# Embedding gathers on GpSimd: a memset between them against a wait for every fourth landing

## Chip, cores, metric

One core of a Trainium2 chip runs the kernel. The metric is the device time of one execution in microseconds (us). Engines are named as in the profile: PE is TensorE (PEld its weight loads), DVE is VectorE, ACT is ScalarE, POOL is GpSimd, SP is SyncE, which only issues DMAs here.

## What is computed

```python
e = jnp.stack([tbl_f[ids[:, f]] for f in range(32)], axis=1)   # [2048, 32, 64] fp32
gram = jnp.einsum('bnd,bmd->bnm', e, e)                         # 32 x 32 products a sample
z = gram[:, rows, cols]                                         # the 496 pairs above the diagonal
h = jnp.concatenate([z, dense_ctx], axis=1)                     # [2048, 512]
h = jnp.maximum(h @ W_top1 + b_top1, 0.0)                       # 512 -> 512
h = jnp.maximum(h @ W_top2 + b_top2, 0.0)                       # 512 -> 256
y = h @ W_top3                                                  # 256 -> 1
```

The 32 tables have 1000, 1250, 12500 or 125000 rows of 64 floats (256 bytes).

## The kernel before

The batch of 2048 is cut into 8 supers (`SUPERS`) of 256 samples, each of two tiles of 128. The 32 fields are sorted into slots by table size. Slots 0 to 15 (`LOOKED_UP`, `UNITS` = 16) have small tables: they stand in SBUF, and each field of a super is looked up on PE, as a product of a one-hot matrix with the table (`look_up`, L303). DVE makes the one-hot matrix (`make_onehot`, L495, a comparison of two fp16 inputs) and adds the three parts of the result (`add_parts`, L503). Slots 16 to 31 are gathered from HBM by GpSimd: one indirect DMA brings 128 rows of 256 bytes, one a partition, so a field of a super takes two. In super 0 slots 12 to 15 are gathered too. That makes 40 gathers for super 0 and 32 for each of the seven others, 264 in all, in the order super, slot, tile, written out without a loop register. All of them are issued by one function, `gather` (L247 to L260), on GpSimd's own instruction stream, which does nothing else until the last 6 moves of cells at the end (L192).

The looked-up and the gathered rows of a super lie in `rows`, which has two halves, for even and odd supers. Slots form 8 groups of 4; a gathered group has 8 gathers (4 slots of 2 tiles) and a semaphore for each half, `rows_landed[parity][group]`, to which each gather adds 16 as it lands. PE's `transpose_group` (L289) waits for the group's whole count. From super 2 on, GpSimd waits ahead of the first gather of each group until the transposes of two supers earlier have been drained (`turned_drained`).

In each step PE transposes the 8 groups of super s, with look-ups for super s + 1 between them, then makes 8 batches of pair products (`gram_batch`, L316), with more look-ups between them and the three layers (L328, L338, L345) of super s - 1. ACT drains the transposes (L404) and the first half of each batch (L441); DVE drains the second half (L530). In the first 60 us DVE and ACT also split the small tables into three bf16 parts (L539, L544, L450), while SP loads those tables. The last super has no look-ups beside it, and after it the layers of the last two supers stand alone.

Between two gathers stands a memset of `pause`, 128 x 384 floats that nobody reads. It adds one to the semaphore `paused`; before it stands a wait until the memset before has been counted.

Of the kernel before, what the change touches and what calls it, by code (L numbers as in the profile page):

```python
# [10 lines left out]
P = 128  # L11
# [9 lines left out]
GROUP_F = 4  # L21
GROUPS = FIELDS // GROUP_F
# [30 lines left out]
READY_MADE = 3  # L53
assert READY_MADE < RING and READY_MADE <= UNITS and not any(GRAM_UNITS[GRAM_BATCHES - READY_MADE + 1:])
SP_MOVES = 10
PAUSE = 384
MOVES = [(i, jq) for i in range(QUAD) for jq in range(QUAD)]
LAYER1_BEFORE, LAYER2_BEFORE, LAYER3_BEFORE = (4, 5), 6, 7

# [31 lines left out]
def build(nc, ids, tables, dense, w1, b1, w2, b2, w3, identity, second, looked_ids, codes, out):  # L91
    fp32, i32, bf16, fp16 = mybir.dt.float32, mybir.dt.int32, mybir.dt.bfloat16, mybir.dt.float16
# [4 lines left out]
    with ctx:  # L97
        def sb(name, shape, dt):
            return ctx.enter_context(nc.sbuf_tensor(name, shape, dt))
# [4 lines left out]
        def sem(name):  # L104
            return ctx.enter_context(nc.semaphore(name))
# [6 lines left out]
        h1 = sb("h1", [P, OT1, SUPER], fp32)  # L112
        h2 = sb("h2", [P, OT2, SUPER], fp32)
        y = sb("y", [1, BATCH], fp32)
        pause = sb("pause", [P, PAUSE], fp32)
        w1_sb = sb("w1_sb", [P, CHUNKS, HIDDEN1], fp32)
        w2_sb = sb("w2_sb", [P, OT1, HIDDEN2], fp32)
        w3_sb = sb("w3_sb", [P, OT2], fp32)
# [30 lines left out]
        rows_landed = [[sem(f"rows_landed_{p}_{g}") for g in range(GROUPS)] for p in range(2)]  # L149
# [31 lines left out]
        onehot_ready = sem("onehot_ready")  # L181
        lookup_ready = sem("lookup_ready")
        looked_up = sem("looked_up")
        paused = sem("paused")
        folds_begun = sem("folds_begun")
        block = ctx.enter_context(nc.Block())

# [3 lines left out]
        def move_cells(engine, i, jq, parity):  # L191
            return engine.dma_start(pairs[FIELDS * jq:FIELDS * (jq + 1), parity, i],  # L192
                                    folded[FIELDS * i:FIELDS * (i + 1), i, CHUNKS * jq:CHUNKS * (jq + 1), :])
# [48 lines left out]

        @block.gpsimd
        def _(pool):
            pauses = count()

            def gather(s, begin=UNITS):  # L247
                for slot in range(begin, FIELDS):
                    f = SLOT_FIELD[slot]
                    if s >= 2 and (slot == begin or slot % GROUP_F == 0):  # L250
                        pool.wait_ge(turned_drained, EMPTY + GROUPS * (s - 2) + slot // GROUP_F + 1)
                    for t in range(TILES):
                        nc.gpsimd.indirect_dma_start(  # L253
                            rows[:, s % 2, slot, t, :], None, tables[f][:, :],
                            bass.IndirectOffsetOnAxis(index[:, s, t, f:f + 1], 0),
                        ).then_inc(rows_landed[s % 2][slot // GROUP_F], 16)
                        before = next(pauses)
                        if before:
                            pool.wait_ge(paused, before)
                        nc.gpsimd.memset(pause[:], 0.0).then_inc(paused, 1)  # L260

            pool.wait_ge(first_index_loaded, 16)
            gather(0, begin=FIRST_UNITS)
            pool.wait_ge(index_loaded, 16)
            for s in range(1, SUPERS):
                gather(s)
            pool.wait_ge(second_copied, GRAM_EMPTY + GRAM_BATCHES * SUPERS)
            for i, jq in MOVES[SP_MOVES:]:
                move_cells(pool, i, jq, 1).then_inc(moved_by_pool, 16)
# [340 lines left out]
```

## Time and profile before

| | |
|---|---|
| median of 3 runs | 508.75 us (504.62 to 510.11) |
| profiled execution, its own time | 506.08 us |
| its span, first to last instruction | 504.3 us |
| busy: PE, DVE, ACT, POOL | 423.6, 297.8, 114.6, 417.8 us |
| gathers on POOL (L253) | 264, 299.4 us |
| memsets on POOL (L260) | 264, 115.7 us |

A busy time is a sum over the instructions of an engine. The span is what the rows of the trace cover; the execution's own time is 1.8 us longer. All durations of the argument come from that one execution, whose own time lies 2.7 us below the median.

### The profile page before, as it was taken

Reading aid. Unit: us, or ns where it says so; the run is one execution under the profiler, and the core shown is the slowest. Engines: PE = TensorE matmul, PEld = TensorE weight load, DVE = VectorE, ACT = ScalarE, POOL = GpSimd, SP = SyncE. Lnnn points to the kernel's source line nnn. Section 1 sums busy time; section 2 is a strip of 40 time slices with the busy share of each in tenths; the row PEclk is TensorE's granted clock in tenths of the full one; section 3 lists DMA queues with packets and bytes.
Section 4 is the critical chain, followed back from the end, with each engine's and each line's share of the span. In section 5 each row is a group of like instructions: output and inputs, shape, how many; then the busy total and the mean of one; then the engine's idle time right before and its main releaser. Section 6 shows DMA issues by size and latency. Waiting matters only on the chain.

```text
span 504.3 us, 10183 instructions
## 1 busy us (share of the span) xinstructions
PE 423.6 (84%) x4080; PEld 382.6 (76%) x4080; DVE 297.8 (59%) x361; ACT 114.6 (23%) x206; POOL 417.8 (83%) x538
## 2 busy tenths in 40 slices
PE   5398589995299989979799969988999959993887
PEld 5387479984298879869698869868897949883765
DVE  2599779794094589448483749339753948250400
ACT  2244312131011321123012311132103300230311
POOL 7999999998898899888998989889998899885010
PEclk9699799997599999999799979999899979996999
DMA  4444631012301122112301123112311231111010
GB/s 109 140 141 149 205 137 22 17 33 51 102 15 23 25 60 98 22 26 61 102 17 24 40 57 88 22 27 56 102 21 21 54 84 44 24 35 44 1 43 2
DMA packets 22070, 29.58 MB, mean 59 GB/s; under 512 B 9910, under 2 KB 14198, under 8 KB 20896
## 3 DMA queue, kind: packets, MB, share of 16 engines
q1 hardware_dynamic: 12980, 18.96, 10.9%
q0 software_dynamic: 8640, 8.86, 10.7%
q10 hardware_dynamic: 404, 1.09, 0.5%
q8 instruction: 37, 0.61, 0.5%
q14 instruction: 9, 0.07, 0.0%
HBM read 24.61 MB, written 0.07 MB: 49 GB/s over the span
## 4 chain that ended last, share of the span: by engine, by line
POOL 82%; issue 9%; PE 4%; DMA 2%; SPq 1%; DVE 1%; ACT 1%; DVEq 0%; ACTq 0%
POOL rows L253 59%; POOL pause L260 23%; PE mlp_ps L328 1%; PE gram_ps L316 1%; SPq L192 1%; PE mlp_ps L338 1%; DVE folded L530 1%; ACT folded L441 0%; DMA rows<-tbl,index 0%; PE gram_ps L352 0%; SPq L219 0%; DMA index<-ids 0%; DMA pairs<-dense 0%; DMA pairs<-folded 0%; PE turn_ps L289 0%
## 5 line engine op out<-in xcount | busy, mean ns | idle before, releaser
L253 POOL DMA_INDIRECT rows<-tbl,index x264 | 299.4, 1134 | 45.9 <-issue 43.3
L303 PE MATMUL turn_ps<-split_sb,onehot 125*128 125x192 bf16 x2192 | 210.4, 256 | 19.9 <-DVE split_sb L544 17.3
L303 PEld LDWEIGHTS turn_ps<-split_sb,onehot 125*128 125x128 bf16 x2192 | 192.9, 102 | 27.8 <-DVE split_sb L544 18.7
L495 DVE TENSOR_TENSOR onehot<-place,codes_wide 125x2048 bf16<-125x2048 f16 (+1 forms) x127 | 168.1, 1325 | 7.3 <-DMA place<-ids_scratch 7.3
L260 POOL MEMSET pause<- 128x384 f32 x264 | 115.7, 438 | 0.2
L503 DVE TENSOR_REDUCE rows<-turn_ps 128x128 f32<-128x384 f32 x124 | 68.8, 556 | 70.8 <-PE turn_ps L303 68.1
L530 DVE COPY_PREDICATED folded<-second_sb,gram_ps 128x512 f32<-128x512 int32 x64 | 46.6, 729 | 81.8 <-ACT folded L441 81.7
L316 PE MATMUL gram_ps<-emb_t 64*128 64x128 f32 x1024 | 74.0, 286 | 3.3 <-DVE folded L530 3.3
L316 PEld LDWEIGHTS gram_ps<-emb_t 64*128 64x128 f32 x1024 | 62.7, 190 | 17.7 <-issue 13.3
L289 PE MATMUL mlp_ps<-ident_sb,rows 128*128 128x128 f32 x240 | 39.1, 288 | 40.8 <-DMA rows<-tbl,index 34.5
L441 ACT COPY folded<-gram_ps 128x512 f32<-128x512 f32 x64 | 37.5, 586 | 152.0 <-PE gram_ps L316 152.0
L289 PEld LDWEIGHTS mlp_ps<-ident_sb,rows 128*128 128x128 f32 x240 | 27.7, 147 | 43.9 <-issue 41.7
L404 ACT COPY emb_t<-mlp_ps 128x512 f32<-128x512 f32 x58 | 34.0, 586 | 114.3 <-PE mlp_ps L289 106.1
L328 PE MATMUL mlp_ps<-pairs,w_sb 128*128 128x256 f32 x256 | 58.5, 383 | 1.1 <-DMA pairs<-dense 1.1
L328 PEld LDWEIGHTS mlp_ps<-pairs,w_sb 128*128 128x128 f32 x256 | 47.5, 190 | 8.3 <-DMA pairs<-dense 1.6
L352 PE MATMUL gram_ps<-ident_sb 128*128 128x128 f32 x192 | 29.2, 316 | 4.3 <-DMA ident_sb<-identity 4.3
L352 PEld LDWEIGHTS gram_ps<-ident_sb 128*128 128x128 f32 x192 | 26.8, 167 | 4.3 <-DMA ident_sb<-identity 4.3
L338 PE MATMUL mlp_ps<-h,w_sb 128*128 128x256 f32 x128 | 29.6, 384 | 0.0
L421 ACT ACTIVATE h<-mlp_ps,b_sb 128x256 f32<-128x256 f32 x32 | 13.4, 471 | 60.0 <-PE mlp_ps L328 60.0
L338 PEld LDWEIGHTS mlp_ps<-h,w_sb 128*128 128x128 f32 x128 | 23.7, 190 | 3.8
L486 DVE COPY y<-mlp_ps 1x256 f32 (+1 forms) x8 | 5.0, 620 | 23.3 <-PE mlp_ps L345 23.3
L192 POOL DMA_DIRECT2D pairs<-folded x6 | 3.0, 525 | 17.2 <-DVE folded L530 17.2
(28 smaller groups left out, 75.8 us busy)
## 6 DMA issues: line engine op xcount, KB each, us to landing
place<-ids_scratch SPq DMA_DIRECT2D x8, 1000.0 KB
rows<-tbl,index POOLq DMA_INDIRECT x264, 2.7
pairs<-folded SPq DMA_DIRECT2D x122, 32.0 KB
emb_t<-tbl SPq DMA_DIRECT2D x8, 250.0 KB
folded<-tbl SPq DMA_DIRECT2D x5, 312.5 KB
w_sb<-w SPq DMA_DIRECT2D x1, 1024.0 KB
place<-ids_scratch ACTq DMA_DIRECT2D x1, 750.0 KB
rows<-tbl SPq DMA_DIRECT2D x2, 312.5 KB
```

The source lines that it names most:

```text
L253: nc.gpsimd.indirect_dma_start(rows[:, s % 2, slot, t, :], None, tables[f][:, :], bass.IndirectOffsetOnAxis(index[:, s, t, f:f + 1], 0),). ...
L260: nc.gpsimd.memset(pause[:], 0.0).then_inc(paused, 1)
L289: last = nc.tensor.transpose(turn_bank[g % banks][:, k, :], rows[:, parity, GROUP_F * g + k].rearrange("p t d -> p (t d)"), ident_sb[:])
L303: last = nc.tensor.matmul(turn_ps[:, u % 2].rearrange("p k b -> p (k b)")[:, t * PARTS * DIM:(t + 1) * PARTS * DIM], onehot[:, u % RING, c ...
L316: last = nc.tensor.matmul(gram_ps[:, k % 2, t, u // TILES].rearrange("p h ij -> p (h ij)"), e.rearrange("p b f -> p (b f)"), e.rearrange(" ...
L328: last = nc.tensor.matmul(mlp_ps[:, o // 2, o % 2, :], w1_sb[:, jj, P * o:P * (o + 1)], pairs[:, parity, :, jj, :], start=(jj == 0), stop= ...
L338: last = nc.tensor.matmul(mlp_ps[:, 0, o, :], w2_sb[:, k, P * o:P * (o + 1)], h1[:, k, :], start=(k == 0), stop=(k == OT1 - 1))
L352: nc.tensor.transpose(gram_ps[:, 0, 0].rearrange("p u h ij -> p (u h ij)")[:, 0:P], ident_sb[:], ident_sb[:])
L441: nc.scalar.copy(folded[:, :, :, BATCH_Q * k:BATCH_Q * (k + 1)].rearrange("p i j (q t) -> p (i j) q t", t=TILES), gram_ps[:, k % 2, :, :, ...
L495: nc.vector.tensor_tensor(onehot[:, u % RING, 0:SPAN[u], :], place[:, parity, u, :].unsqueeze(1).to_broadcast([TP, SPAN[u], SUPER]), codes ...
L503: nc.vector.reduce_sum(rows[:, parity, u, :, :], turn_ps[:, u % 2].rearrange("p k b -> p (k b)")[:, 0:TILES * PARTS * DIM] .rearrange("p ( ...
L530: nc.vector.copy_predicated(folded[:, :, :, BATCH_Q * k:BATCH_Q * (k + 1)].rearrange("p i j (q t) -> p (i j) q t", t=TILES), second_sb[:]. ...
```

## The change

The memset, its tile and its semaphore are gone. GpSimd counts its gathers, and behind every fourth (`AT_ONCE`) it waits until the group's semaphore has all that has been issued to it so far. As every group has 8 gathers, the four gathers behind one another always belong to one group, and the wait asks for the landing of all four. There are 66 such waits, 10 in super 0 and 56 behind it.

```diff
-PAUSE = 384
+AT_ONCE = 4
...
-        pause = sb("pause", [P, PAUSE], fp32)
...
-        paused = sem("paused")
...
-            pauses = count()
+            issued = count()
+            landed = [[0] * GROUPS for _ in range(2)]
...
                         ).then_inc(rows_landed[s % 2][slot // GROUP_F], 16)
-                        before = next(pauses)
-                        if before:
-                            pool.wait_ge(paused, before)
-                        nc.gpsimd.memset(pause[:], 0.0).then_inc(paused, 1)
+                        group = slot // GROUP_F
+                        landed[s % 2][group] += 1
+                        if next(issued) % AT_ONCE == AT_ONCE - 1:
+                            pool.wait_ge(rows_landed[s % 2][group], 16 * landed[s % 2][group])
```

## Rows read from the trace of the kernel before

**Rows 1.** The page: chain that ended last, shares of the span by engine and line

```profile
POOL 82%; issue 9%; PE 4%; DMA 2%; SPq 1%; DVE 1%; ACT 1%; DVEq 0%; ACTq 0%
```

**Rows 2.** The chain in order of time: start, us, what; its begin and its last gather

```profile
0.75 1.95 DMA index<-ids
2.70 0.29 issue
2.99 1.15 POOL rows L253
...
459.62 2.36 DMA rows<-tbl,index
461.98 0.04 issue
462.02 1.12 PE turn_ps L289 x4
```

**Rows 3.** The page, costliest groups: busy us, mean ns, idle before and its releaser

```profile
L253 POOL DMA_INDIRECT rows<-tbl,index x264 | 299.4, 1134 | 45.9 <-issue 43.3
L260 POOL MEMSET pause<- 128x384 f32 x264 | 115.7, 438 | 0.2
L192 POOL DMA_DIRECT2D pairs<-folded x6 | 3.0, 525 | 17.2 <-DVE folded L530 17.2
```

**Rows 4.** PE's waits from 75 to 470 us: us in total, times, longest us

```profile
PE mlp_ps L289 <- DMA rows<-tbl,index: 34.5, 7, 10.8
PE turn_ps L289 <- DMA rows<-tbl,index: 7.7, 1, 7.7
```

**Rows 5.** PE's wait for rows in two stretches, 180:190 and 350:356 us

```profile
PE mlp_ps L289 <- DMA rows<-tbl,index: 2.4, 1, 2.4
...
PE mlp_ps L289 <- DMA rows<-tbl,index: 2.3, 1, 2.3
```

**Rows 6.** Timeline of POOL, a stretch without DVE one-hots: start, us, instruction, [idle before]

```profile
321.33 0.95 POOL L253 DMA_INDIRECT rows<-tbl,index  x1 [0.17 <-issue]
322.28 0.43 POOL L260 MEMSET pause<- 128x384 f32 x1
322.88 0.95 POOL L253 DMA_INDIRECT rows<-tbl,index  x1 [0.17 <-issue]
```

**Rows 7.** Timeline of DVE and POOL from 141 to 147 us, large one-hots

```profile
141.04 1.48 DVE L495 TENSOR_TENSOR onehot<-place,codes_wide 125x2560 bf16<-125x2560 f16 x1
141.48 0.43 POOL L260 MEMSET pause<- 128x384 f32 x1
142.08 1.27 POOL L253 DMA_INDIRECT rows<-tbl,index  x1 [0.16 <-issue]
...
143.80 1.48 DVE L495 TENSOR_TENSOR onehot<-place,codes_wide 125x2560 bf16<-125x2560 f16 x1
143.94 2.16 POOL L253 DMA_INDIRECT rows<-tbl,index  x1 [0.17 <-issue]
```

**Rows 8.** Timeline of POOL: first and last of 81 gathers behind 75 us over 1.06 us

```profile
80.31 1.16 POOL L253 DMA_INDIRECT rows<-tbl,index  x1 [0.17 <-issue]
...
425.13 1.27 POOL L253 DMA_INDIRECT rows<-tbl,index  x1 [0.17 <-issue]
```

**Rows 9.** Gathers of super 0 and then of the others, by tile: min/median/max

```profile
L253 POOL DMA_INDIRECT rows<-tbl,index x40: 950/961/2032, 3.0 to 73.9; - x40
DMA to landing us min/median/max: 3.9/4.6/6.2
...
L253 POOL DMA_INDIRECT rows<-tbl,index x224: 950/952/2258, 75.5 to 459.6; - x112
DMA to landing us min/median/max: 2.3/2.5/3.6
```

**Rows 10.** L253 by windows: stretch, POOL busy (gathers), TensorE clock, DMA share, GB/s

```profile
0.00:75.00 75.00, 47.61 (x40) 0.89 0.47 148
75.00:461.00 386.00, 251.82 (x224) 0.94 0.20 46
```

**Rows 11.** Timeline of DVE and POOL from 343 us, one one-hot of 1.2 us a turn

```profile
343.20 1.21 DVE L495 TENSOR_TENSOR onehot<-place,codes_wide 125x2048 bf16<-125x2048 f16 x1
343.48 0.43 POOL L260 MEMSET pause<- 128x384 f32 x1
344.08 1.16 POOL L253 DMA_INDIRECT rows<-tbl,index  x1 [0.17 <-issue]
...
344.96 1.22 DVE L495 TENSOR_TENSOR onehot<-place,codes_wide 125x2048 bf16<-125x2048 f16 x1
345.24 0.43 POOL L260 MEMSET pause<- 128x384 f32 x1
345.84 1.16 POOL L253 DMA_INDIRECT rows<-tbl,index  x1 [0.17 <-issue]
```

## Prediction

> **What bounds the kernel now.** I read the chain that ended last first: 82% of the span is POOL and 9% issue, PE only 4% [rows 1]. Its parts in order of time show what that is: GpSimd starts when the indices have landed, at 2.99 us, and from there to the last gather at 459.62 us the chain never leaves it. Only then follow the landing, PE's last group and a tail of 42 us in which no gather takes part [rows 2]. The groups say the same: 299.4 us of gathers, 115.7 us of memsets, and 45.9 us of idle time before the gathers, of which 43.3 us are "issue", no releaser [rows 3]. GpSimd waits for nobody, neither for a free half of `rows` nor for anything else. PE, at 84% of the span the busiest engine, waits for rows in each step: 34.5 + 7.7 us in 8 waits behind 75 us [rows 4]. So each microsecond on GpSimd between 3 and 460 us is one of the kernel, as long as PE keeps a wait. The shortest of those waits are 2.4 and 2.3 us [rows 5], the others 4.2 to 10.8 us.
>
> The timeline of POOL shows the period: gather 0.95, memset 0.43, 0.17 us of nothing before the next gather, 1.55 us together [rows 6]. That 0.17 stands ahead of practically all gathers (43.3 us over 263). The mean gather is longer than 0.95, 1.134 us. Beside DVE one sees why: the gather at 142.08 takes 1.27 us and the one at 143.94 takes 2.16, and both end about 0.95 us behind the point at which a one-hot is all but over (142.4 and 145.15, where the one-hots of 1.48 us end at 142.52 and 145.28) [rows 7]. A gather that meets a one-hot at its begin stands still until that is done, and then takes its 0.95. 97 of the 264 gathers are longer than 1.06 us, 16 of them in super 0 and 81 behind it [rows 8]; all stalls together are 299.4 - 264 x 0.95 = 48 us.
>
> **The change, term by term.** All terms lie on GpSimd's own stream, so they add up.
>
> Memsets out: 263 x 0.438 us (the last has no gather behind it) = -115.3 us.
>
> Waits in: a wait ends when the four gathers behind one another have landed. The landing is read from the start of a gather: median 4.6 us in super 0 (3.9 to 6.2), 2.5 us behind it (2.3 to 3.6) [rows 9]. Super 0 runs while the tables are being loaded: DMA share 0.47 against 0.20 afterwards [rows 10]. From that I take off what GpSimd works anyway, the gather: 47.61/40 = 1.19 us in super 0 [rows 10], 0.95 us behind it. Then the restart: the first gather stands 0.29 us behind the landing of its indices [rows 2], and that holds the 0.17 which is there today, so 0.12 are new. A wait costs 4.6 - 1.19 + 0.12 = 3.53 us in super 0 and 2.5 - 0.95 + 0.12 = 1.67 us behind it. With 10 waits and 55 (the last wait has no gather behind it) that is 35.3 + 91.9 = +127.2 us.
>
> Queued behind a waiting GpSimd are only the next gathers, and for these waits PE's transposes; the six moves at the end come 17 us after the last gather [rows 3], so they don't feel it.
>
> The gap of 0.17 us ahead of a gather that follows a gather directly: before shows no such pair, so it is bounded. From above by the 0.17 us ahead of every gather now; from below by the six direct DMAs on the same engine, 3.0 us for six of 0.525 each [rows 3], no gap at all. I take 0.17, since it is the same instruction, and nothing that the memset does shows in it. The other end is worth -0.17 x 198 = -33.7 us (three of four gathers follow one directly), and a gather that meets a one-hot takes nothing of it, so about -33.7 x 167/264 = -21 us.
>
> The stalls at one-hots: the waits take GpSimd off the road for a quarter of the time behind super 0 (91.9 of 386 us), and a one-hot that falls there costs nothing: up to 38.6 (the late stalls, 251.8 - 224 x 0.952) x 0.24 = -9 us. The other way, without the memset a gather arrives earlier and waits longer for the same end. Where one-hots come in turns, GpSimd passes one gather a turn: 344.08, 345.84, every 1.76 us like the one-hots [rows 11]. Between 0.95 + 0.17 and 0.95 + 0.43 + 0.17 us the turn makes no difference. 81 late gathers are stalled; three in four don't stand behind a wait, 61 x 0.438 = +27 us at most, if each was in a turn. Several are not, and each turn lost also puts gathers behind the one-hots, where they are free. I take 0 for both together, and keep -9 and +27.
>
> Here a rule of the Trainium skill speaks against the change: SBUF — State Buffer, the section on the bandwidth-pool intuition, has a DMA issued by GpSimd blocked until the VectorE operation ends, about 115 ns more, because the port pair is locked. By that rule memsets inside a turn are free, and taking them out saves nothing there; the term of +27 us would hold in full. The trace agrees for gathers. [...]
>
> Landing with four in flight: gathers come 1.12 us apart instead of 1.55. In super 0 the data of a gather may queue: at worst the DMA side needs the present 1.55 us for each, so the fourth lands up to 3 x 0.43 = 1.3 us later, 10 x 1.3 = +13 us. I take 0, as the landings stay near 4.6 us through super 0 without growing.
>
> Sum: -115.3 + 127.2 = +11.9 us. In super 0 alone the change costs 35.3 - 40 x 0.438 = +18 us; behind it, it gains 6. On the profiled execution: 506.08 + 11.9 = 518.0 us, and with the 2.7 us by which that lies under the median, 520.7; I say 520. PE has no part in it: its waits grow.
>
> **The rivals.**
> 1. *No gap between gathers* (faster). The mechanism is the pair of gathers back to back, the place all 198 of them, the price -21 to -34 us: 520.7 - 21 = 500 to 487, likeliest 498 as most of the stalls remain. It speaks for it that the direct DMAs on POOL show none [rows 3] and that the memset starts the instant a gather ends [rows 6]; against it, that the gap is ahead of each gather whatever stalled the one before. It turns the sign as soon as the gap is under 0.17 - 11.9/(198 x 0.63) = 0.07 us. PE's waits would still cover it, as 10 us over 8 steps are under the 2.3 us of the tightest.
> 2. *In between* (no change that can be measured): a gap of 0.05 to 0.12 us, or waits that swallow more stalls; 504 to 513 us. No row speaks for it but the width between the two ends.
> 3. *The turns decide* (slower than forecast): the +27 us, or the queue in super 0: 520 + 13 to 520 + 27, 533 to 547 us. For it: the even 1.76 us [rows 11]. Against it: a wait that ends inside a turn costs less than its 1.67 us, because there was slack.
> 4. *A landing before the wait*: the change would not wait at all if the four had landed already. The earliest landing, 2.3 us after its start [rows 9], is 1.35 us behind the gather's end, so this can't be; every wait holds.
>
> **How the numbers follow.** Chances: forecast 0.42, rival 1 0.30, rival 2 0.18, rival 3 0.10. A measurement of this kernel tells 1%, 5.1 us, from no change: faster is under 503.7, slower over 513.8. That gives faster 0.31, same 0.19, slower 0.50. Forecast's own range is 512 to 530. Over all, cut at 1 in 10 on each side, 493 to 536: the lower bound leaves out the end of rival 1 near 487, the upper one the far half of rival 3.
>
> **What would show it.** On POOL: 66 waits with DMA rows as releaser, of about 3.5 us in super 0 and 1.7 behind it, some 127 us together (a sum with the 0.17 of each, so up to 138 as idle time); the start of super 1's first gather near 75.5 + 18 = 94 us; the last gather near 459.6 + 12 = 471 us; the tail of 42 us as before; mean gather still near 1.13 us. The start-to-start distance of two free gathers, 1.12 or 0.95, settles rival 1 at once. A mean gather of 1.25 or more says rival 3. I am wrong if that distance is short, if landings in super 0 come sooner once GpSimd issues in bursts, or if the restart takes well over 0.29 us: each 0.1 us there is 6.6 us of the kernel.

## The result: 13% slower

The changed kernel takes 573.12 us (median of 4 runs, 567.71 to 575.99) against 506.69 us before (4 runs): a ratio of 1.130, interval 1.118 to 1.142. The forecast was 520 us, range 493 to 536: the sign was right, the size far off. The profiled execution took 573.93 us, its span is 572.1 us. Where executions of a kernel fall into two groups more than 1.5% apart, the ratio is that of the faster group, while the median is of all of them.

The page of the changed kernel, the chain by engine and the two groups that answer to [rows 1] and [rows 3]:

```profile
POOL 41%; DMA 24%; issue 19%; PE 12%; SPq 1%; DVE 1%; ACT 1%; POOLq 0%; DVEq 0%; ACTq 0%
...
L252 POOL DMA_INDIRECT rows<-tbl,index x264 | 313.1, 1186 | 213.9 <-DMA rows<-tbl,index 149.4
L190 POOL DMA_DIRECT2D pairs<-folded x6 | 3.0, 520 | 17.1 <-DVE folded L529 17.1
```

GpSimd still sets the end, now together with the DMA that it waits for. The gathers have become 13.7 us longer (299.4 before), their idle time has grown from 45.9 to 213.9 us, and 115.7 us of memsets are gone. Its waits (us in total, times, longest):

```profile
POOL rows L252 <- DMA rows<-tbl,index: 149.4, 64, 5.5
POOL rows L252 <- issue: 60.3, 198, 0.3
...
POOL rows L252 <- ACT emb_t L403: 1.8, 1, 1.8
```

Two lines to read closely. The second is the surprise: 198 gathers that stand directly behind another one have 60.3 us ahead of them, 0.30 us each, not 0.17. The first has 64 waits; the 65th stands in the third line, where by the trace the free buffer came a little later than the landing. The timeline of POOL shows both kinds of distance, and a long wait:

```profile
303.94 0.94 POOL L252 DMA_INDIRECT rows<-tbl,index  x1 [1.73 <-DMA rows<-tbl,index]
305.18 0.95 POOL L252 DMA_INDIRECT rows<-tbl,index  x1 [0.30 <-issue]
...
409.27 0.94 POOL L252 DMA_INDIRECT rows<-tbl,index  x1 [5.49 <-DMA rows<-tbl,index]
```

From start to start a free gather takes 1.24 to 1.25 us, against 1.55 with a memset of 0.43 us between [rows 6]. So the memset had cost 0.30 us a gather, not 0.44: 0.13 us of it lay in time that a gather needs ahead of it anyway.

The chain's last gather answers to [rows 2]:

```profile
526.53 2.43 DMA rows<-tbl,index
528.96 0.04 issue
529.01 1.12 PE turn_ps L288 x4
```

The first gather starts at 2.87 us, the last at 526.53, 67.0 us more between them than before (459.62 less 2.99). The tail behind the last gather is 45.6 us against 44.7. PE has no share in the difference: its waits for rows, 42.2 us before [rows 4], are 90.4 us now, over the whole span:

```profile
PE mlp_ps L288 <- DMA rows<-tbl,index: 79.7, 10, 12.4
...
PE turn_ps L288 <- DMA rows<-tbl,index: 10.7, 2, 8.7
```

The balance on GpSimd, by the rows above and [rows 3]: waits 149.4 + 1.8, direct gaps 60.3, less the 43.3 us of gaps before, less 115.3 of memsets, plus 13.7 of longer gathers, makes +66.6 us of the 67.0.

### The profile page after: what moved, and what is told of

The parts are those of the page before. It is cut to its first block, busy times and chain, and to the rows that moved or that the text cites. A ratio compares the mean times of both kernels' runs of the same rounds, so it can differ in the third digit from the quotient of the medians.

```text
span 572.1 us, 9945 instructions
## 1 busy us (share of the span) xinstructions
PE 435.4 (76%) x4080; PEld 388.2 (68%) x4080; DVE 295.4 (52%) x361; ACT 113.9 (20%) x206; POOL 316.3 (55%) x274
## 4 chain that ended last, share of the span: by engine, by line
POOL 41%; DMA 24%; issue 19%; PE 12%; SPq 1%; DVE 1%; ACT 1%; POOLq 0%; DVEq 0%; ACTq 0%
POOL rows L252 41%; DMA rows<-tbl,index 23%; PE turn_ps L302 4%; PE mlp_ps L327 3%; PE gram_ps L315 3%; PE mlp_ps L337 1%; SPq L190 1%; PE mlp_ps L288 1%; DVE folded L529 1%; ACT folded L440 0%; PE gram_ps L351 0%; SPq L217 0%; PE mlp_ps L344 0%; DMA pairs<-dense 0%; DMA pairs<-folded 0%
## 5 line engine op out<-in xcount | busy, mean ns | idle before, releaser
L252 POOL DMA_INDIRECT rows<-tbl,index x264 | 313.1, 1186 | 213.9 <-DMA rows<-tbl,index 149.4
L302 PE MATMUL turn_ps<-split_sb,onehot 125*128 125x192 bf16 x2192 | 217.2, 260 | 26.8 <-DVE split_sb L543 17.1
L302 PEld LDWEIGHTS turn_ps<-split_sb,onehot 125*128 125x128 bf16 x2192 | 197.1, 104 | 38.4 <-DVE split_sb L543 18.5
L288 PE MATMUL mlp_ps<-ident_sb,rows 128*128 128x128 f32 x240 | 41.6, 301 | 86.5 <-DMA rows<-tbl,index 79.7
L288 PEld LDWEIGHTS mlp_ps<-ident_sb,rows 128*128 128x128 f32 x240 | 29.1, 154 | 90.9 <-issue 65.8
L327 PE MATMUL mlp_ps<-pairs,w_sb 128*128 128x256 f32 x256 | 60.3, 391 | 1.1 <-DMA pairs<-dense 1.1
L327 PEld LDWEIGHTS mlp_ps<-pairs,w_sb 128*128 128x128 f32 x256 | 48.7, 194 | 9.0 <-DMA pairs<-dense 1.6
L420 ACT ACTIVATE h<-mlp_ps,b_sb 128x256 f32<-128x256 f32 x32 | 13.5, 472 | 53.1 <-PE mlp_ps L327 48.5
L426 ACT ACTIVATE h<-mlp_ps,b_sb 128x256 f32<-128x256 f32 x16 | 6.7, 472 | 24.0 <-PE mlp_ps L337 24.0
```

The costliest lines, as they stand in the source:

```text
L252: nc.gpsimd.indirect_dma_start(rows[:, s % 2, slot, t, :], None, tables[f][:, :], bass.IndirectOffsetOnAxis(index[:, s, t, f:f + 1], 0),). ...
L288: last = nc.tensor.transpose(turn_bank[g % banks][:, k, :], rows[:, parity, GROUP_F * g + k].rearrange("p t d -> p (t d)"), ident_sb[:])
L302: last = nc.tensor.matmul(turn_ps[:, u % 2].rearrange("p k b -> p (k b)")[:, t * PARTS * DIM:(t + 1) * PARTS * DIM], onehot[:, u % RING, c ...
L327: last = nc.tensor.matmul(mlp_ps[:, o // 2, o % 2, :], w1_sb[:, jj, P * o:P * (o + 1)], pairs[:, parity, :, jj, :], start=(jj == 0), stop= ...
```

## Experiments

All were timed in three rounds beside the kernel before, whose median was 505.0 to 505.6 us each time. "After" is the changed kernel.

### 1. Neither memset nor wait

```diff
-                        if next(issued) % AT_ONCE == AT_ONCE - 1:
-                            pool.wait_ge(rows_landed[s % 2][group], 16 * landed[s % 2][group])
```

> After, without its 66 waits: neither memset nor wait. Theory (the waits cost 1.5 us and more each, the gap between two gathers is 0.30 us and not 0.17): gathers start 1.25 us apart, with stalls 1.45 on average, the last one near 2.9 + 264 x 1.45 = 386 us, so PE no longer waits for rows and sets the time: 506.7 less the 42 us of such waits, about 465 us. Rival (the pauses or waits protect something: with more gathers in flight each gather or its landing gets slower): gathers over 1.5 us each or landings over 5 us behind 75 us, and no less than 500 us in total.

466.61 us, ratio 0.923 (0.918 to 0.928): the theory's number. The page's chain and group of this kernel, and its waits on PE:

```profile
PE 44%; POOL 27%; SPq 13%; issue 8%; DMA 6%; DVE 1%; ACT 1%; DVEq 0%; ACTq 0%
...
L252 POOL DMA_INDIRECT rows<-tbl,index x264 | 337.0, 1276 | 82.6 <-issue 78.6
```

```profile
PE turn_ps L298 <- DVE split_sb L539: 19.6, 5, 10.9
PE mlp_ps L284 <- issue: 6.1, 2, 3.1
PE turn_ps L284 <- DMA rows<-tbl,index: 5.4, 1, 5.4
```

PE leads the chain and waits for rows 5.4 us in all. The gathers are the longest of any kernel here, 1276 ns on average: a faster GpSimd meets more one-hots, as rival 3 of the prediction had it, but with PE as the bound that costs nothing. After is 106 us slower than this kernel, and only its 66 waits are between the two. So far it looked as if the memset of before had been mere loss. Experiment 6 shows that it isn't so simple.

### 2. Memset and waits together

```diff
+                        before = next(pauses)
+                        if before:
+                            pool.wait_ge(paused, before)
+                        nc.gpsimd.memset(pause[:], 0.0).then_inc(paused, 1)
                         if next(issued) % AT_ONCE == AT_ONCE - 1:
```

> Before, with the 66 waits of after added behind the memsets. Theory (waits are dear by themselves: 2.16 us idle on average behind super 0, about 3.4 in it, of which a memset and its 0.17 us hide 0.61): 55 x 1.55 + 10 x 2.8 = +113 us, about 620 us. Rival (the time of after comes from gathers standing directly behind one another, by gap and stalls, and a wait costs no more than the 1.67 us less a hidden memset that was forecast): 55 x 1.24 + 10 x 2.9 = +97 us, 604 us or less.

617.28 us, ratio 1.223 (1.213 to 1.232). The theory's 620 holds. Its gathers:

```profile
L256 POOL DMA_INDIRECT rows<-tbl,index x264 | 299.4, 1134 | 155.4 <-DMA rows<-tbl,index 120.3
```

The idle time is 109.5 us more (155.4 less 45.9), and the kernel 111.7. That the mean gather is the same as before to the nanosecond (1134) is a coincidence of two effects: the 40 gathers of super 0 take 53.8 us against 47.6, and the 224 others 245.7 against 251.8 [rows 10]. So the waits by themselves, on the kernel before, cost some 112 us, and what was given for them, the memset, is worth 617.3 - 573.1 = 44 us, not 115. The two pages say where the rest of the 115.7 went: without the memsets GpSimd is idle for 58.5 us more (213.9 against 155.4), and its gathers take 13.7 us more.

### 3. A memset of one column, with the waits

```diff
-PAUSE = 384
+PAUSE = 1
```

In the kernel of experiment 2.

> After with a memset of one column instead of none behind each gather, waits as in after. Theory (a gather needs about 1.25 us from start to start whatever short thing stands between; the memset of 384 columns was worth only 0.30 of its 0.44 us): start to start 1.22 to 1.25 us and 573 us within 1%. Rival (the 0.30 us and the long stalls in super 0, 20 us against 9.5, come from a gather directly behind a gather): the gap ahead of a gather is 0.17 us, stalls in super 0 near 10 us, 560 us or less.

574.61 us, as after. Its timeline of POOL:

```profile
103.67 0.94 POOL L256 DMA_INDIRECT rows<-tbl,index  x1 [0.19 <-issue]
104.62 0.11 POOL L263 MEMSET pause<- 128x1 f32 x1
104.92 0.94 POOL L256 DMA_INDIRECT rows<-tbl,index  x1 [0.19 <-issue]
```

0.11 + 0.19 is 0.30 again, and 1.25 from start to start. In no kernel here did a gather start within 0.30 us of the end of the one before it; a short memset fits into that for nothing. In super 0 the stalls were 20 us here too, so the rival falls in both its parts.

### 4. Waits at eight, and what makes a wait long

```diff
-AT_ONCE = 4
+AT_ONCE = 8
```

> After with a wait behind every eighth gather: 33 waits in place of 66. Theory (each wait costs its idle time less the 0.30 us gap: 1.86 us behind super 0, about 3.1 in it): 28 x 1.86 + 5 x 3.1 = 68 us less, 505 us. Rival (a landing late because of other transfers is waited for however seldom one asks; or eight in flight land later): less than half of that, 540 us or more.

521.01 us, ratio 1.027 (1.018 to 1.037), between the two. GpSimd's idle time fell by 66.6 us (147.3 against 213.9), near the 68 expected, but its gathers grew by 14.1 (327.2 against 313.1): what isn't waited is in part stalled at one-hots. 66.6 - 14.1 = 52.5, and 52.1 were measured.

Next, the refill of `place`, 1000 KB of SP's queue in each step, cut to 64 KB in after:

```diff
-                sp.dma_start(place[:, parity], scratch.ap()[bass.ds(of, 1)].to_broadcast([TP, UNITS, SUPER])
+                sp.dma_start(place[:, parity, 0:1], scratch.ap()[bass.ds(of, 1), 0:1].to_broadcast([TP, 1, SUPER])
```

> After, with SP's refill of place from super 2 on cut to the first of its 16 fields (64 KB instead of 1000 KB each; the other fields keep the samples of two supers earlier, so what they look up is left as it was). Theory (six of the waits behind super 0 take 4 to 5.5 us instead of 1.8, since the fourth landing falls into the refill): those six come down by 2.9 us each, 17 us in all, about 556 us. Rival (the long landings come from the moves of pairs or from the tables in HBM themselves): the same six places stay above 3 us and the time at 573 us.

554.81 us (545.72 to 560.58), ratio 1.085 (1.076 to 1.093) where after has 1.130, so 18 us less by the medians and 23 by the ratios. GpSimd's waits for landings behind super 0 (and the one ahead of super 1), first of after, then of this kernel:

```profile
POOL rows L252 <- DMA rows<-tbl,index: 118.6, 55, 5.5
```

```profile
POOL rows L252 <- DMA rows<-tbl,index: 101.6, 56, 3.1
```

To the 55 of after belongs the one of 1.8 us that stands in the line of the free buffer: 120.4 us against 101.6 for 56 waits. That is 18.8 us less. Seven waits of after took 3.4 to 5.5 us, here only one takes over 3 (3.1): the refills were behind the long waits.

### 5. Stalls and super 0

In after, the one-hots of supers 2 to 7 are replaced by a memset of one column of one block (but for the first three of each super):

```diff
+                if not first and loads is None and not isinstance(s, int):
+                    nc.vector.memset(onehot[:, u % RING, 0:1, 0:1], 0.0).then_inc(onehot_ready, 1)
+                    return
```

> After, with the one-hot matrices of fields 3 to 15 of supers 2 to 7 left out: DVE writes one column of one block instead and signals as before, so the look-ups take old matrices. Theory (a gather that meets a one-hot at its begin stands still until it ends): of the 36 us of stalls behind the first gather of super 2 some 30 go, about 543 us, and gathers there take 0.95 us each but for those beside the three one-hots left. Rival (the long gathers come from the DMA side or PE): stalls stay, 573 us.

540.06 us, 33 less than after. The gathers from super 2 on, in windows of after and then of this kernel (stretch, GpSimd busy and count, clock, DMA share, GB/s):

```profile
164.00:530.00 366.00, 217.43 (x192) 0.92 0.18 41
```

```profile
156.00:500.00 344.00, 190.54 (x192) 0.95 0.18 44
```

26.9 us of 192 gathers are gone: 0.99 us each instead of 1.13. Of the rest of the 33 us, 4 came in super 0, which the edit doesn't touch (super 1 started 4 us earlier); where the others came from was not followed. That a gather stands still at DVE's one-hots, read from the timeline alone in [rows 7], is shown by this. The Trainium skill, SBUF — State Buffer, on the bandwidth-pool intuition, says of a DMA that GpSimd issues beside a copy on VectorE that it is "blocked until DVE-end + ~115 ns"; that the comparison with two inputs does the same is shown by the runs here. The 115 ns more are not seen: the two stalled gathers of [rows 7] end 0.83 us behind the one-hot's end, less than the 0.95 us that a free one takes. In the trace of after one case goes beyond the end of the operation. DVE and POOL in super 0:

```profile
23.19 1.22 DVE L494 TENSOR_TENSOR onehot<-place,codes_wide 125x2048 bf16<-125x2048 f16 x1
23.46 5.31 POOL L252 DMA_INDIRECT rows<-tbl,index  x1 [5.29 <-DMA rows<-tbl,index]
24.33 0.69 DVE L538 TENSOR_TENSOR pairs<-emb_t,split_sb 125x512 f32<-125x512 f32 x1
...
27.27 0.69 DVE L543 TENSOR_TENSOR split_sb<-pairs,split_sb 125x512 bf16<-125x512 f32 x1
...
27.87 0.55 DVE L502 TENSOR_REDUCE rows<-turn_ps 128x128 f32<-128x384 f32 x1
```

This gather let six two-input operations pass and got in at the reduction, 0.95 us ahead of its own end. In before and in the six kernels without waits in super 0 no gather of super 0 was passed over like this at a border of two such operations; in the nine kernels with waits in super 0 it happened at 9 to 17 borders in each. Why a landing wait makes that difference stays open. In after it comes to some 10 us of stalls in super 0.

Then the waits of after in super 0 and behind it, each alone:

```diff
-                        if next(issued) % AT_ONCE == AT_ONCE - 1:
+                        if next(issued) % AT_ONCE == AT_ONCE - 1 and s >= 1:
```

> After, with its waits only from super 1 on (56 of 66). Theory (super 0 is a term by itself: without waits its 40 gathers end near 62 us as in the kernel without any, instead of 102): the first gather of super 1 at 62 us, 573 - 40 = 533 us. Rival (what GpSimd is late by in super 0 is partly made up later, where PE or the buffers would have held it): 545 us or more.

541.04 us in the median, but in two pairs: 534.05 and 536.54, near the theory, 545.54 and 546.53, at the rival. So 27 to 39 us of the time of after are super 0's, and it is no clean test: PE is starved from 27 to 66 us in it (the profiled execution, 536.54), as described under the next kernel. For this kernel and two of the next (one column without waits, one column behind super 0) no ratio is given, as their executions lie 2 to 6% apart.

```diff
-                        if next(issued) % AT_ONCE == AT_ONCE - 1:
+                        if next(issued) % AT_ONCE == AT_ONCE - 1 and s == 0:
```

> After, with its waits only in super 0 (10 of 66). Theory: the 40 gathers end near 102 us; afterwards GpSimd is faster than PE, which stays late by what it waits in step 0 and 1, so 466.6 + 36 to 40 = about 504 us. Rival (PE had slack in super 0, as the split of the tables holds it up anyway): 485 us or less. If the long stalls in super 0 belong to the waits, they are here (20 us) and not in the kernel with waits behind super 0 (9 us).

659.02 us, ratio 1.300 (1.293 to 1.307). Both expectations fall. With 56 waits fewer the kernel is 86 us slower than after. The timeline of PE:

```profile
240.97 0.37 PE L315 MATMUL gram_ps<-emb_t 64*128 64x128 f32 x1 [1.52 <-issue]
241.68 0.37 PE L315 MATMUL gram_ps<-emb_t 64*128 64x128 f32 x1 [0.34 <-issue]
243.78 0.37 PE L315 MATMUL gram_ps<-emb_t 64*128 64x128 f32 x1 [1.73 <-issue]
245.87 0.37 PE L315 MATMUL gram_ps<-emb_t 64*128 64x128 f32 x1 [1.72 <-issue]
```

PE has no wait between two products of a batch in the program, and yet it issues one in 2.1 us where 16 take 1.16. I call this starved. There were six such stretches, from 152, 231, 299, 372, 419 and 531 us on. All but the fifth began inside a row of gathers 1.25 us apart without a stall (the fifth just ahead of one), and each ended 4 to 7 us behind the start of the last gather of its row. The trace of before has none, that of after four single gaps of 0.3 to 0.8 us between two products, 1.9 us together. The kernel without one-hots has 20 of these gaps, 10.5 us together, although no row of gathers in it is longer than four.

A slow fetch of instructions is not what the trace shows. Queue 8 in the pages of before and of this kernel:

```profile
q8 instruction: 37, 0.61, 0.5%
```

```profile
q8 instruction: 37, 0.61, 0.4%
```

Each of these 37 transfers took 0.9 to 1.5 us in before and 0.9 to 1.6 here, and none ran between 230 and 265 us, in which the stretch shown lies.

### 6. What the memset is good for

The same kernel, waits only in super 0, with a memset behind each gather from super 1 on, first of 384 columns, then of one.

```diff
+PAUSE = 384
...
+                        if s >= 1:
+                            before = next(pauses)
+                            if before:
+                                pool.wait_ge(paused, before)
+                            nc.gpsimd.memset(pause[:], 0.0).then_inc(paused, 1)
```

> The kernel with waits only in super 0, with the memset of 384 columns back behind each gather from super 1 on. In that kernel (659 us) PE issued one product every 2.1 to 2.8 us in seven stretches, without waiting for a semaphore, each time GpSimd had issued some 8 to 14 gathers 1.25 us apart without a stall. Theory (that unbroken pace starves PE): with 1.55 us from start to start no such stretch; super 1 starts at 102 us as in after, and from there 384 us to the last gather and 46 of tail as before, 533 us. Rival (the waits in super 0 leave a state that slows PE later): such stretches stay, over 600 us.

528.93 us, ratio 1.048 (1.042 to 1.055), against an expected 533; short slow places are left near 262 and 322 us, with gaps of 0.3 to 0.4 us inside a batch.

```diff
-PAUSE = 384
+PAUSE = 1
```

> As the run before it in this list, with a memset of one column. Theory (the pace counts: 1.25 us from start to start whether one column is written between or nothing): PE is starved in the same places, over 600 us. Rival (any instruction between two gathers lets PE's instructions through, whatever the pace): about 504 us, the sum that was expected of waits in super 0 alone.

669.12 us (651.90 to 691.94), with long starved stretches. So an instruction between two gathers doesn't keep PE from being starved; at the slower pace of the 384 columns it nearly stays away. Then memsets of one, 192 and 288 columns in the kernel before, with no waits anywhere:

```diff
-PAUSE = 384
+PAUSE = 1      # then 192, then 288
```

> Before with a memset of one column instead of 384. Theory (what lies under 0.30 us between two gathers costs nothing): start to start of free gathers 1.24 to 1.25 us as without any memset, 467 us. Rival (a memset of any length costs its own 0.11 us and 0.17 us of gap on top, or keeps PE's instructions coming): another distance, and a time over 470 or under 463 us.

665.79 us (637.70 to 675.39). The distance of 1.25 us is as the theory has it, the time is 199 us off: PE is starved again, from 31 to 106 us and in six later stretches.

> Before with a memset of 192 columns instead of 384, some 0.22 us shorter. Theory (the time falls with GpSimd's distance until PE sets it): start to start 1.33 to 1.35 us, about 264 x 1.5 = 400 us for all gathers, and PE sets the time, 467 to 475 us. Rival (the time of before is not GpSimd's pace but its number of gathers in flight): over 490 us.

585.04 us, ratio 1.160 (1.151 to 1.169), distance 1.39 us, PE starved in part. The rival's number held, and not by its mechanism.

> Before with a memset of 288 columns, GpSimd's distance 1.47 us against 1.55 (384 columns, 505 us) and 1.39 (192 columns, 585 us). Theory (starving sets in by distance, between 1.39 and 1.55): either still free of it, then 264 x 0.08 = 21 us less than before, 484 us, or in it, over 520 us. Rival (the time rises steadily as the memset is shortened, because something else is slowed): about 540 us with no starved stretch of PE.

494.43 us, ratio 0.977 (0.973 to 0.980): the first version beside experiment 1 that beats before, 10 us behind the expected 484, as its gathers are 13.5 us longer. Its timeline of POOL, 1.47 us from start to start:

```profile
200.09 0.95 POOL L253 DMA_INDIRECT rows<-tbl,index  x1 [0.16 <-issue]
201.04 0.35 POOL L260 MEMSET pause<- 128x288 f32 x1
201.56 0.96 POOL L253 DMA_INDIRECT rows<-tbl,index  x1 [0.17 <-issue]
```

No starved stretch there. So among the kernels without waits PE was starved at 1.39 us and not at 1.47. What remains is experiment 1, which goes at 1.25 us and is free of it:

```diff
-                        before = next(pauses)
-                        if before:
-                            pool.wait_ge(paused, before)
-                        nc.gpsimd.memset(pause[:], 0.0).then_inc(paused, 1)
+                        if not next(pauses):
+                            nc.gpsimd.memset(pause[:], 0.0).then_inc(paused, 1)
```

> Neither waits nor memsets, but for one memset of 384 columns behind the first gather, which moves all later gathers by 0.3 us or less. Theory (whether PE is starved depends on where an unbroken row of gathers falls, not on the code): a time of its own, over 500 us at least in some of the runs, with stretches of starved PE. Rival (a kernel without memsets between its gathers is free of it, the small memsets bring it): 467 us as the kernel with neither.

467.23 us, ratio 0.922 (0.918 to 0.926), no starved stretch: the rival. But the rival can't be the whole of it, for the kernel with waits only in super 0 has no memset either, and the one with waits behind super 0 has up to gather 40 the same stream on GpSimd as experiment 1, and is starved from 27 us on. What can be read is that in experiment 1 and in this last kernel no unbroken row is longer than 13 gathers, since PE and DVE keep pace and a one-hot breaks it, while in the starved ones rows of 21 to 29 occur: a starved PE makes DVE idle, so no one-hot stalls a gather, so the row goes on. That would explain why the state holds once it is there; no run tested it, and the 20 gaps beside rows of four say that a long row is not needed for a short one. What starts it, and which resource PE lacks, stays open. One rival is untested: every execution here was recorded by the profiler. The traces without one gap of more than 0.25 us inside a batch of PE (before, experiments 1 to 3, the wait at eight, 288 columns, this last kernel) hold 7700 to 8100 updates of semaphores, all others, after with them, only 4500 to 5400. So records are missing just where PE had such gaps, and a share of the recording in them is not excluded.

## Why the prediction was wrong

**What bounds the kernel.** Right: GpSimd to its last gather before and after, PE with waits that only grew.

**The gap between two gathers.** This is the step that failed first and cost most: the 0.17 us taken for a gather that follows a gather. I bounded it by 0.17 us from above, "since it is the same instruction, and nothing that the memset does shows in it", and took 0.17. It is 0.30, outside both ends: 60.3 us for 198 gaps where the sum had 33.7, so +26.6 us. The error was to read "0.17 us ahead of a gather" as a property of the gather alone. Part of what it needs lay under the memset, where no row shows it; experiment 3 finds 0.11 + 0.19 for the same 0.30. The upper bound should have reached to memset and gap together, 0.60 us. Rival 1 (no gap) falls by the same rows.

**Memsets out.** The 115.3 us are right as busy time, but only 44 us is what the memset was worth beside waits (experiment 2): 0.13 us of each now stands as gap, what it hid of a landing is waited for (151.2 us of waits against 120.3 in experiment 2), and the gathers are 13.7 us longer.

**The waits.** Mechanism right, 65 waits held; size too small: 151.2 us where 127.2 + 65 x 0.17 = 138.2 stood, +13 us. In super 0 the forecast was too high (30.8 + 1.7 = 32.5 us for ten, against 37.0), and its one price for ten waits hid two. Five took 4.2 to 5.3 us, up to 67.5 us, and the five behind them 1.7 to 1.8, against 3.70 forecast for each. The tables are loaded by then: the DMA share is 0.52 from 30 to 62 us and 0.12 from 72 to 102. The first waits had pushed the second half of super 0 out of the load, in which the landings of [rows 9] were taken. Behind super 0 the forecast was too low (118.7 against 101.2). There the median wait is 1.77 us, against 1.84 forecast, but the mean is 2.16, because seven waits took 3.4 to 5.5 us. I had taken the median of the landings, 2.5 us, with the maximum of 3.6 in the same row [rows 9]; a sum over 55 waits needs the mean, and a wait for four landings needs the latest of four. Experiment 4 shows whose landings those are.

**The restart** of 0.29 us was right: the chain of after has 0.26 us of it behind a landing (303.68 to 303.94), and the common wait is 1.73 to 1.77 us of idle time.

**Stalls.** I took 0 between -9 and +27; the gathers grew by 13.7 us, 10.1 of it in super 0 (57.7 against 47.6), where the trace of before gave no hint. Behind it the two effects nearly cancelled, as assumed: 255.4 - 251.8 = 3.6 us. Experiment 2 separates them: adding the waits took 6.1 us off the late gathers (forecast up to 9), and taking the memsets out put 9.7 us back (forecast at most 27). Rival 3 had the right direction with a fraction of its price. So the term of +27 us did not hold in full, only by about a third.

**Four in flight.** 0 was nearly right. During the load the five waits of after come to 4.76 us each from the gather's end, those of experiment 2, where gathers stay 1.55 us apart, to 4.04 us and a memset of 0.43. The closer pace is worth 0.3 us each, 1.5 us in all at most.

**Sum.** 26.6 + 13.0 + 13.7 = 53.3 us of the 54.7 by which GpSimd came out later than forecast (67.0 against 11.9, less rounding). Three terms all erred on one side, and the range had been cut as if only one would. That the waits in super 0 came out within 5 us of their forecast is luck: five were 5.3 us dearer together, five 9.8 us cheaper.

## What to carry to other kernels

When an instruction between two others is taken out, the gap left behind is unknown and may be longer than the one beside it: bound it from above by all that stood there, and test with the shortest stand-in. A wait for a landing behind every few small DMAs costs the DMA's completion time each time (2.4 us from issue here, of which only 0.94 is GpSimd's work), and over many waits its mean counts, with the long ones beside bulk transfers. Look for a useless instruction's second effect before striking it: here the memset of 384 columns kept GpSimd's pace, 288 gave 2.3% and 192 lost 16%. And equal means before and after can hide two effects, so split them by stage.

## What the runs showed of the hardware

- Two gathers of 128 rows on GpSimd started no closer than 1.24 us in any kernel here, 0.94 of it the instruction; direct DMAs of 32 rows follow one another without a gap (0.52 us each).
- While GpSimd issues gathers 1.25 to 1.39 us apart without a break, PE can fall to one product in 2.1 or 2.8 us, with no semaphore in the way. Four kernels with no or few waits took 585 to 669 us with it, and it stayed away in two others of the same pace (467 us). At 1.47 us, and at 1.55 in before, it was not seen; at 1.55 us behind a super 0 with waits, gaps of 0.3 to 0.4 us were left. Whether it exists without the profiler is not known.
- A gather that meets a two-input comparison on DVE at its begin stands still until it ends; without those of supers 2 to 7, but for three of each, 192 gathers took 26.9 us less. A memset on GpSimd inside such a comparison took its 0.43 us as ever [rows 7].
- A gather that meets a chain of two-input operations on DVE was kept out for up to 4.4 us (a record of 5.3), but only in kernels whose GpSimd waited for landings in that stretch.
